# A mixture-of-experts kernel on one core: two layout changes move from TensorE to VectorE blocks plus regrouping transfers

## The reference

```python
L, H, NH, NKV, HD, FF, E, K = (4, 256, 16, 4, 64, 512, 8, 2)
for l in range(L):
    res = x
    h = _attention(_rms(x, ln1_w[l]), wq[l], wk[l], wv[l], wo[l], cos, sin, causal_bias)
    x = jnp.clip(res + h, -100.0, 100.0)
    x = jnp.clip(x + _moe(_rms(x, ln2_w[l]), wr[l], wg[l], wu[l], wd[l]), -100.0, 100.0)

def _moe(x, wr, wg, wu, wd):
    topv, topi = jax.lax.top_k(jax.nn.softmax(x @ wr, axis=-1), K)
    ...
    for e in range(E):
        h = jax.nn.silu(x @ wg[e]) * (x @ wu[e])      # [tokens, 512]
        out = out + comb[..., e:e + 1] * (h @ wd[e])  # [tokens, 256]
```

## Time and profile before

| | |
|---|---|
| median of 3 runs | 1965.41 us (1962.46 to 1965.87) |
| the profiled execution | 1962.85 us, of which 1961.0 us from the first to the last instruction (the span); 1.85 us lie around it |
| PE busy | 1894.9 us, 97% of the span, 11088 matmul records |
| DVE, ACT, POOL busy | 1181.4 us (60%), 1007.9 us (51%), 536.9 us (27%) |
| chain of waits that ended last | PE 76%, DVE 9%, ACT 7%, POOL 3%, issue 3%, DMA 1% |
| mean granted TensorE clock | 0.993 of full |
| DMA | 88760 packets, 149.39 MB, mean 76 GB/s; SP's queue busy 18.5% of 16 engines' span |

### The profile page before, as it was taken

The page is one execution under the profiler, slowest core; times in us unless marked ns, Lnnn a source line. Parts: engine busy times, 40 slices in busy tenths (PEclk is TensorE's granted clock), DMA queues, the critical chain, the costliest instruction groups (busy, mean ns, idle before and its releaser), DMA issues.

```text
span 1961.0 us, 36294 instructions
## 1 busy us (share of the span) xinstructions
PE 1894.9 (97%) x11088; PEld 1409.5 (72%) x11089; DVE 1181.4 (60%) x2901; ACT 1007.9 (51%) x3741; POOL 536.9 (27%) x704
## 2 busy tenths in 40 slices
PE   6999999999999999999999999999999999999994
PEld 5887887766668888766667888766667888766662
DVE  4676778543357888643357878643356888653345
ACT  4646776632336677632335766733335776642331
POOL 3752113340022322440022232440022333430023
PEclk9999999999999999999999999999999999999997
DMA  6422320231112330231121430231121340131123
GB/s 160 125 69 103 102 93 15 78 94 43 56 57 87 112 116 4 82 96 43 54 61 58 144 112 6 81 93 46 46 68 57 117 143 6 50 101 47 49 72 101
DMA packets 88760, 149.39 MB, mean 76 GB/s; under 512 B 13346, under 2 KB 64244, under 8 KB 88500
## 3 DMA queue, kind: packets, MB, share of 16 engines
q1 hardware_dynamic: 74664, 112.85, 18.5%
q0 software_dynamic: 13568, 34.27, 5.9%
q10 hardware_dynamic: 380, 0.38, 0.1%
HBM read 105.87 MB, written 41.59 MB: 75 GB/s over the span
## 4 chain that ended last, share of the span: by engine, by line
PE 76%; DVE 9%; ACT 7%; POOL 3%; issue 3%; DMA 1%; SPq 0%; POOLq 0%; DVEq 0%; ACTq 0%
PE ps L859 25%; PE ps L878 12%; PE ps L749 7%; ACT parena L1179 7%; PE ps L829 6%; PE ps L805 4%; PE ps L868 3%; PE ps L779 3%; PE ps L794 3%; PE ps L757 2%; PE ps L731 2%; POOL qk L547 2%; DVE rope L1499 2%; PE ps L853 2%; DVE rope L1503 2%
## 5 line engine op out<-in xcount | busy, mean ns | idle before, releaser
L859 PE MATMUL ps<-arena,xeT 128*128 x1120 | 527.9, 594 | 0.0
L1179 ACT ACTIVATE parena<-ps,nmax 112x112 f32<-112x112 f32 x1024 | 345.4, 389 | 105.3 <-DVE nmax L1520 105.3
L859 PEld LDWEIGHTS ps<-arena,xeT 128*128 128x128 f32 x1120 | 203.0, 192 | 141.6 <-issue 134.4
L547 POOL TENSOR_TENSOR qk<-qk,rope 128x448 f32<-128x448 f32 x128 | 146.3, 1143 | 555.1 <-DVE rope L1503 554.9
L1228 ACT ACTIVATE parena<-ps,er 128x512 f32<-128x512 f32 x140 | 96.2, 687 | 379.0 <-PE ps L859 375.5
L749 PE MATMUL ps<-xnT,wqk_s 128*128 128x224 f32 x1280 | 273.6, 357 | 0.0
L878 PE MATMUL ps<-arena,tarena 128*128 x1120 | 266.0, 380 | 1.9 <-issue 1.2
L526 POOL DMA_INDIRECT y_in<-sorted_y,pos x114 | 111.8, 980 | 543.9 <-DMA sorted_y<-tarena 402.3
L1179 ACT ACTIVATION_READ_ACCUMULATOR parena<-ps,nmax 112x1 f32 x1024 | 247.4, 242 | 0.0
L829 PE MATMUL ps<-wo_s,oT 128*112 128x256 f32 x1024 | 237.9, 385 | 1.4 <-issue 1.4
L749 PEld LDWEIGHTS ps<-xnT,wqk_s 128*128 128x128 f32 x1280 | 233.2, 191 | 2.9
(11 more groups left out here) (185 smaller groups left out, 2731.7 us busy)
## 6 DMA issues: line engine op xcount, KB each, us to landing
xe<-sorted_x SPq DMA_DIRECT2D x140, 130.0 KB, 2.1
sorted_y<-tarena SPq DMA_DIRECT2D x140, 128.0 KB
arena<-in_L_ffn_wg_dram SPq DMA_DIRECT2D x32, 512.0 KB, 3.7
arena<-in_L_ffn_wu_dram SPq DMA_DIRECT2D x32, 512.0 KB, 4.6
arena<-in_L_ffn_wd_dram SPq DMA_DIRECT2D x32, 512.0 KB, 5.5
arena<-in_ctx_dram SPq DMA_DIRECT2D x15, 375.0 KB
sorted_x<-tarena POOLq DMA_DIRECT2D x8, 568.8 KB, 4.5
qk<-in_L_ffn_wq_dram SPq DMA_DIRECT2D x4, 1024.0 KB
```

The costliest lines, as they stand in the source:

```text
L547: pool.tensor_tensor(q, q, rope[m % 2][:, :], ALU.add).then_inc(g_rope, 1)
L859: last = pe.matmul(ps[:, bank, :], xeT[u][:, k, :], w[:, bass.ds(e * 1024 + k * 512, 512)], start=(k == 0), stop=(k == KD - 1))
L1179: last = act.activation(prob[:, n, :], ps[0:S, bank, h * S:h * S + S], ACT.Exp, bias=nmax[:, b % 2, n:n + 1], scale=SCALE, accum_out=rsum[ ...
```

## The change

Token rows: `turn_tile` moves from PE to DVE, as one 32x32 block transpose of 128x256. A block transpose turns each 32x32 block in place and doesn't move blocks between partition groups, so `load_tile` now regroups while it loads: four DMAs, each with 32 partitions times 4 runs of 64 floats. The load brings 256 columns, and the two factors come by a DMA of their own (`load_factors`, 128 runs of 2 floats). ACT's `copy_tile` becomes `scale_tile`, from SBUF to SBUF in place.

Intermediate rows: for tiles 0 to EARLY-1 = 3 and the last one (34), `turn_hidden` and `copy_hidden` stay. For the other 30, DVE's `blocks` transposes 128x512 in 32x32 blocks into `hidB`; ACT's queue issues four stores to the DRAM scratch `hid_d` (`store_hidden`, each 32 partitions times 8 runs of 64 floats) and, once all four have landed, one load back (`load_hidden`, 128 partitions times 2 runs of 256 floats). `down` reads that, now two tiles behind `up`. `wd` is loaded in the matching row order (2 runs of 512 floats a partition in place of one of 1024). `hid` has one buffer.

```diff
-                    sp.dma_start(xe[u], sorted_x[bass.ds((NT - 1) * SLOT - T * SLOT, SLOT), :]).then_inc(ld_xe[u], 16)
+                    for c in range(4):
+                        src = sorted_x[bass.ds((NT - 1) * SLOT - T * SLOT, SLOT), 64 * c:64 * c + 64]
+                        sp.dma_start(xe[u][32 * c:32 * c + 32, :].rearrange("j (r x) -> j r x", r=4),
+                                     src.rearrange("(r j) x -> j r x", r=4)).then_inc(ld_xe[u], 16)
+
+                def load_factors(T, u, peeled=False):
+                    if not peeled:
+                        sp.wait_ge(m_h, l * NT + T - 1)
+                        alone(sp)
+                    sp.dma_start(er[:, u, :], sorted_x[bass.ds((NT - 1) * SLOT - T * SLOT, SLOT), D + 1:D + 3]).then_inc(ld_er[u], 16)
...
                         if not (first and u == 0):
-                            store_tile(i * 2 + u - 1, 1 - u)
+                            load_factors(i * 2 + u + 1, 1 - u)
+                        if not first:
+                            store_tile(i * 2 + u - 2, u)
...
                         up(T, u, e, wg_s, 2 * u, m_g)
-                        turn_hidden(T - 1, 1 - u)
+                        if isinstance(T, int) and T <= EARLY:
+                            turn_hidden(T - 1)
...
-                    if not end:
-                        turn_tile(T + 1, 1 - u, n)
...
-                    down(T - 1, 1 - u, expert_of(T - 1))
+                    if isinstance(T, int) and T <= EARLY:
+                        down(T - 1, 1 - u, None, expert_of(T - 1))
+                    elif not (isinstance(T, int) and T == EARLY + 1):
+                        down(T - 2, u, n - 1 - u - EARLY // 2, expert_of(T - 2))
...
+                def store_hidden(T, u, n):
+                    act.wait_ge(m_z, l * 2 * HID + T - EARLY + 1)
+                    alone(act)
...
+                    for r in range(4):
+                        act.dma_start(hid_d[u][:, :, r, :].rearrange("h (c i) x -> i (h c) x", c=4),
+                                      hidB[u][32 * r:32 * r + 32, :].rearrange("i (g x) -> i g x", g=8)).then_inc(st_hid[u], 16)
+
+                def load_hidden(T, u, n):
+                    act.wait_ge(st_hid[u], l * HID * 64 + n * 64 + 64)
+                    alone(act)
...
+                    act.dma_start(hidG[u].rearrange("p (h x) -> p h x", h=2),
+                                  hid_d[u].rearrange("h p r x -> p h (r x)")).then_inc(ld_hid[u], 16)
...
+                def turn_tile(T, u, n):
+                    dve.wait_ge(ld_xe[u], l * 64 * TILES[u] + n * 64)
+                    if not (isinstance(T, int) and T < 2):
+                        dve.wait_ge(m_u, l * NT + T - 1)
+                    alone(dve)
+                    dve.transpose(xeT[u][:, :, :].rearrange("p k (r j) -> p k r j", r=4),
+                                  xe[u].rearrange("p (r i k) -> p k r i", r=4, k=KD)).then_inc(m_r, 1)
...
+                def blocks(T, u, n):
+                    dve.wait_ge(m_h, l * NT + T + 1)
+                    if not (isinstance(T, int) and T < EARLY + 2):
+                        dve.wait_ge(st_hid[u], l * HID * 64 + n * 64)
+                    dve.transpose(hidB[u].rearrange("p (g j w) -> p g w j", g=8, w=2),
+                                  hid.rearrange("p (g i w) -> p g w i", g=8, w=2)).then_inc(m_z, 1)
...
                 def tile(T, u, n, first=False, count=False):
                     hidden(T, u)
-                    copy_factors(T + 1, 1 - u)
+                    if not (isinstance(T, int) and T < EARLY):
+                        blocks(T, u, n - u - EARLY // 2)
+                    if not (isinstance(T, int) and T + 2 >= NT):
+                        turn_tile(T + 2, u, n - u + 2)
...
-                    copy_result(T - 1, 1 - u, n)
+                    if isinstance(T, int) and T <= EARLY:
+                        copy_result(T - 1, 1 - u, n)
+                    elif not (isinstance(T, int) and T == EARLY + 1):
+                        copy_result(T - 2, u, n - u)
```

More of the change, by code:

```diff
@@ L125, in xattn_ffn @@
         res_d = nc.dram_tensor("res_d", [S, B, D], F32, kind="Internal").ap()
+        hid_d = [nc.dram_tensor(f"hid_d{u}", [2, 128, 4, 64], F32, kind="Internal").ap() for u in range(2)]
         arena = sb("arena", [128, 3 * E * KD * FF])
@@ L1024, in layer @@
                     iteration(b)
-                turn_hidden(0, 0)
+                turn_hidden(0)
                 for p in range(2):
@@ L1295, in early, with tile @@
                             copy_in(n, 1, 1, 5, 256)
-                def tile(T, u, first=False, ahead=False, end=False):
-                    tanh(T, u)
+                def tile(T, u, n, first=False, ahead=False, end=False):
+                    tanh(T, u, n)
                     if first:
@@ L1315, in layer @@
                 copy_hidden(0)
-                tile(1, 1, first=True)
-                tile(2, 0)
-                tile(3, 1)
+                tile(1, 1, 1, first=True)
+                tile(2, 0, 2)
+                tile(3, 1, 2)
                 gate_exponents(1)
-                with act.Fori(2, AHEAD // 2) as i:
-                    tile(i * 2, 0)
-                    tile(i * 2 + 1, 1)
+                for T in range(4, EARLY + 2):
+                    tile(T, T % 2, T // 2 + 1)
+                with act.Fori(EARLY // 2 + 1, AHEAD // 2) as i:
+                    tile(i * 2, 0, i + 1)
+                    tile(i * 2 + 1, 1, i + 1)
                 for T in range(AHEAD, NT):
-                    tile(T, T % 2, ahead=not last_layer, end=(T == NT - 1))
+                    tile(T, T % 2, T // 2 + 1, ahead=not last_layer, end=(T == NT - 1))
                 if not last_layer:
@@ L1887 @@
 AHEAD = NT - 9
+EARLY = 4
+HID = (NT - 1 - EARLY) // 2
+assert EARLY % 2 == 0 and EARLY + 2 <= WHOLE
 assert AHEAD > FIRST and AHEAD % 2 == 0
```

130 lines of the change are left out of this document (73 added, 57 removed).

## The result

The changed kernel takes 1993.34 us (median of 4 runs, 1988.77 to 1996.33) against 1965.64 for the kernel before in the same comparison: ratio 1.0147, 95% interval [1.0133, 1.0161]. I had forecast 1954, 11 us faster than before. It is 28 us slower than before and 39 us above the forecast, inside the range of 1915 to 2014, on the side to which I had given 0.39.

The account below looks back on a forecast made before the run. PE was taken to bound the kernel at 5.86 us a loop tile; afterwards the first trip would set 5.7. Gain 86 x (5.86 - 5.7) + 9.6 - 12 = 11 us, so 1954 us, range 1915 to 2014.

Parts of the forecast that it names:

- the side to which I had given 0.39: Whole kernel: the changed kernel comes out slower than the kernel before; chance 0.39, against 0.49 for faster.
- What leaves PE: PE: `turn_tile` leaves for 140 tiles (32 us), `turn_hidden` for 120 (56 us), together 88.6 us.
- the sum 5.16: PE's loop tile without the moved transposes: 5.86 - 0.70 = 5.16 us.
- DVE's transposes: DVE, two block transposes per tile: 0.45 us for 128x256 and 0.70 for 128x512.
- The first trip: Loop, SP and DVE: copy, store, four loads, landing, transpose, next copy; 5.65 us, rounded to 5.7, sets the loop.
- The slower rival: Same SP and DVE trip with load steps of 0.66 us: 6.22 a tile, -33 us, about 1998; chance 0.32.
- The second trip: Loop, ACT: `hid_d` stores, landing, load, then scaling; 10.1 to 10.4 us for two tiles, level with PE.
- The start of the MoE: Opening, tiles 8 and 9: 1.1 us a layer behind and one `down` owed; about -3 us a layer, -12 in all.
- The owed `down`: Opening of each layer: one put-off `down`, 1.7 us, still owed at tile 9.
- The end of the MoE: Tiles from 29 on, layers 0 to 2: six tiles gain up to 0.7 each; 3.2 us a layer, 9.6 in all.
- The rule on the pause: PE at tile 8: half clock after a 6 us pause costs up to 21 us in all; taken as nothing.
- The DMA engines as bound: Rival, loop: 139 packets at 51 ns take 7.1 us a tile, -109 us, about 2074; chance 0.05.

Follow-up runs that it names:

- inter_only: Changed kernel, but token rows come by one load a tile and `turn_tile` stays on PE; 1977.57 us, ratio 1.0078 to the kernel before.
- token_only: Changed kernel, but `turn_hidden` stays on PE for every tile, no `hid_d`, `down` one tile behind; 1965.39 us, ratio 1.0008 to the kernel before.
- load_late: Changed kernel with ACT's load of `hid_d` moved behind the scaling and the next layer's copies; 1986.50 us, ratio 1.0130 to the kernel before.
- all_moved: Changed kernel with factors' load ahead of the store, DVE's token transpose last in its tile, ACT's `hid_d` load behind the scaling; 1945.86 us, ratio 0.9910.
- turn_last: Changed kernel with DVE's transpose of token rows moved behind its routing work and its copy; 1983.27 us, ratio 1.0092 to the kernel before.

## Why the prediction was wrong, point by point

- **What leaves PE.** Right. All `turn_tile` records are gone; single tiles 5.15 to 5.17 apart do occur, as the sum 5.16 has it, but no version's loop reached that mean. (PE lost 760 matmul records, 280 of `turn_tile` and 480 of `turn_hidden`.)
- **DVE's transposes.** Right: 128x256 took 0.445 us (taken 0.45), 128x512 0.712 (taken 0.70).
- **The first trip.** Right in mechanism, place and size: forecast 5.65 to 5.7, measured 5.63, with five issues 6.03. The terms, as means over tiles 12 to 25 of all layers: copy to store 0.20 (taken 0.18), store 0.37 (0.35), store to load 0.63 (0.58), first to fourth load 1.53 (1.41), fourth load's start to the transpose 2.17 (2.2), transpose 0.37 until the copy starts (0.51), copy 0.39 (0.42). None is off by more than 0.14, and the errors cancel. The slower rival lived on steps of 0.66; they took 0.51, so it did not happen, though its side of zero did.
- **The second trip.** In inter_only too short by 1.2 to 1.5 us for two tiles: 11.6, not 10.1 to 10.4 (the terms as I gave them add up to 10.0 to 10.3). The term that was mis-sized most is the landing: 3.15 us from the last store's start to the load, not 2.1 to 2.4; the rest is 0.2 on the way to the transpose's end, 0.3 of wakes before the stores and 0.2 behind the load's issue. It took 26 us in the loop from inter_only, otherwise the best half. In the changed kernel that landing was 2.09, as taken; the way to the transpose's end was 6.04, with slack for the late factors in it. With 5.40 there the trip would be 10.6 and thus, as forecast, under the first one.
- **The first step that failed: "The start of the MoE".** I gave -12 us in all, 1.1 a layer behind at tile 9 and one `down` owed. Tiles 0 to 9 cost 21.7 us, 5.4 a layer, and the owed `down` came on top. I had followed only tile 8's own chain (loads, landing, transpose, scaling: forecast 430.5, measured 433.00) and not what is queued behind its waiting instructions. On SP that is the factors of tile 7, on DVE the copy of tile 4 and, earlier, the routing. Putting the transpose last gave 6 us back in the changed kernel; with the factors early as well it gave 18 in token_only. Before that, at 415.5, the second trip holds PE 2.6 us, but that alone cost nothing: load_late has no such pause and the same 245.1 us, its pause before tile 8 being 6.8 us instead. What is left in all_moved (15 us) is in part the clock, below. `copy_factors` I had counted as a saving; with it went the arrival of a tile's factors together with its rows.
- **The owed `down`.** Right in size (1.7 a layer): between layers the versions with `hid_d` lost 3.9 to 5.7 us, those without gained 3. But the tail paid it once more, 5.3 us, with a wait for `hid_d` before the last `down`.
- **The second step that failed, and the larger: "The end of the MoE".** I gave +9.6 us, and the late tiles not set by PE's next-layer work another 3. They lost 10.7. The 0.7 per plain late tile came; but new waits stand there before other work too. The next layer's copies stood behind the wait for `hid_d` on ACT (3.1 us of PE at tile 29); load_late gave 6.7 back, nothing of it in layer 3. DVE's wait for `xe` stood before its copy; moving it behind (turn_last) gave 13.6 back, 2.9 of it in layer 3. all_moved gave 25.
- **The rule on the pause.** A term that I put at nothing; that was wrong. I went by the first 20 us alone, and didn't look for the rest: the trace of before has one stretch at 0.50 in layer 3's attention, some 2 us behind a pause of 1.00 us. In the changed kernel PE pauses 2.59 us before 418.05, and gate and `up` take 5.39 in place of 3.6. (The rows of the clock are below.) The 21 us that I had named as its upper end are of the right order: it is at most some 15 us here, 10 in the opening and 5 in the late tiles (the estimate above). Here the trace agrees with the Trainium skill (TensorE: Matmul & The Clock Gate, Part 1): an idle TensorE fell to its half rate.
- **The DMA engines as bound.** Didn't happen: in 450 to 500 us they were busy 58%, 19872 packets (rows below). That is 0.584 x 50 x 16 / 19872 = 23.5 ns for one; I had 3.4 us of 5.7 for a tile, 60%, with 20 ns for a short packet. At 51 ns for the 3328 longer packets, the short ones took about 18 ns each (an estimate), so their time does fall with their size, as forecast. The Trainium skill (DMA: Bandwidth & Descriptors, Specifications) wants 512 bytes for full rate; 139 GB/s with most packets under that is no contradiction, and here it decided nothing.

```profile
DMA packets 19872, 6.96 MB, mean 139 GB/s; under 512 B 16544, under 2 KB 19872, under 8 KB 19872
...
q10 hardware_dynamic: 12240, 4.72, 38.0%
q1 hardware_dynamic: 7632, 2.24, 20.4%
```

The granted clock (third number from the end), first in the kernel before and then in the changed one:

```profile
1707.50:1710.70 3.20, 3.20 (x11) 1.08 (x10) 0.17 (x2) 2.19 (x7) 0.00 (x0) 0.50 0.00 0
419.40:422.60 3.20, 3.20 (x5) 1.35 (x4) 0.69 (x1) 0.69 (x1) 2.43 (x3) 0.50 0.73 187
```

In sum: forecast gain 11 us = loop and its like 13.8, late 9.6, opening and owed work -12. Measured in spans -26.0 = first tile 0.3, loop 15.6, opening -21.7, late -10.7, between -4.2, tail -5.3. By the places of the forecast: the 68 tiles of the loop were to gain 10.9 and gained 15.6; opening, `down` between the layers and tail were to cost 12 and cost 31.2; the late tiles were to gain 12.5 and lost 10.7. The loop came out as worked; the two ends, which I had priced from one chain each, were off by 19 and 23 us.

## What to carry to other kernels

When an operation is replaced by a round trip through memory, don't only compute the steady state: for each new wait on an in-order queue, write down what stands behind it in the first and last trips, where that queue also carries other work (routing, the next layer's copies, a small load for an earlier tile). Put the wait last in its engine's tile: here three moves of a few lines turned 1.0147 into 0.9910, and one alone turned 1.0078 into 0.9883. And where two rings are within a few tenths of a microsecond, cutting one changes the loop little or makes it longer (5.63 became 5.63 and 5.78); cut both before judging either (5.48). A pause that a new wait makes on PE is paid twice if the clock falls behind it.

## What the runs showed of the hardware that I had not expected

- After a pause of 5.34 us TensorE ran at a granted clock of 0.50 for some 6 us; after one of 2.59 us at 0.50 from 419.4 to 422.6. The 5.34 us pause thus cost 3.06 more in the tile behind it, the other 1.79.
- A chip can change the sign of a result: the same two kernels gave 1.0147 [1.0133, 1.0161] and 0.9955 [0.9931, 0.9978]. The changed kernel's loop tile agreed to 0.02 us on both; on a third chip like the second, 41 of the 60 us that the kernel before had lost lay in tiles 0 to 9, where PE, ACT and DVE stop at tile 5.
- DMAs issued behind one another start 0.51 us apart on SP (four loads, 1.53 us from the first to the fourth) and 0.46 on ACT (four stores, 1.38), whose next activation started 0.13 us after the last of them.
